# A transformer layer on one core: one pair of loads moved from the end of a stage to its eighth weight block, and the last two tiles of the program accumulated output tile by output tile

## What is computed

```python
h = _ln(x) * (1.0 + sc1) + sh1
x = x + g1 * _gqa_attn(h, wq, wk, wv, wo)     # 16 heads, 4 of keys and values
h = _ln(x) * (1.0 + sc2) + sh2
x = x + g2 * _mlp(h, w1, b1, w2, b2)          # gelu, 512 -> 2048 -> 512
```

## Time and profile before

| | |
|---|---|
| median of 3 runs | 1415.4 us (1413.36 to 1415.44) |
| the profiled execution, its own time | 1418.17 us |
| its span, first to last instruction | 1416.2 us |
| PE busy | 1381.6 us, 98% of the span |
| DVE, ACT, POOL busy | 881.1, 763.5, 641.7 us |

### The profile page before, as it was taken

The page is one execution under the profiler, slowest core; times in us unless marked ns, Lnnn a source line. Parts: engine busy times, 40 slices in busy tenths (PEclk is TensorE's granted clock), DMA queues, the critical chain, the costliest instruction groups (busy, mean ns, idle before and its releaser), DMA issues.

```text
span 1416.2 us, 19196 instructions
## 1 busy us (share of the span) xinstructions
PE 1381.6 (98%) x6681; PEld 991.2 (70%) x6681; DVE 881.1 (62%) x1481; ACT 763.5 (54%) x1375; POOL 641.7 (45%) x279
## 2 busy tenths in 40 slices
PE   6999999999999999999999999899999999999998
PEld 4655565665656566565567878788888888888886
DVE  3687787686777768677665565755475355733243
ACT  6377758576675856667756556534443344422221
POOL 3067687685867768587810085412032010311012
PEclk9999999999999999999999999999999999999999
DMA  8332222423233242323259685476662865546523
GB/s 285 88 90 59 67 92 82 123 78 106 57 91 96 83 117 80 110 57 87 78 165 266 137 277 152 156 253 193 179 193 66 303 189 164 155 156 195 149 82 119
DMA packets 163438, 193.85 MB, mean 137 GB/s; under 512 B 59960, under 2 KB 84552, under 8 KB 163344
## 3 DMA queue, kind: packets, MB, share of 16 engines
q1 hardware_dynamic: 163344, 192.64, 45.3%
HBM read 108.91 MB, written 40.93 MB: 106 GB/s over the span
## 4 chain that ended last, share of the span: by engine, by line
PE 82%; DVE 6%; SPq 3%; DMA 3%; ACT 2%; POOL 2%; issue 1%; DVEq 0%; ACTq 0%; POOLq 0%
PE acc L2388 18%; PE proj_bank L1183 13%; PE turn L2375 9%; PE key_bank L1267 8%; PE pv_bank L1276 7%; PE row_bank L1254 7%; PE up L2375 7%; PE up L1645 4%; PE acc L2339 3%; DVE neg_max L994 2%; PE sum_bank L1286 2%; SPq L559 2%; DMA gate_now<-gate_scratch 1%; POOL probs_sum L689 1%; PE proj_bank L1193 1%
## 5 line engine op out<-in xcount | busy, mean ns | idle before, releaser
L994 DVE TENSOR_REDUCE neg_max<-row_bank 128x1 f32<-128x512 f32 x512 | 337.7, 684 | 139.1 <-PE row_bank L1254 135.2
L818 ACT ACTIVATE probs<-key_bank 128x512 f32<-128x512 f32 x512 | 299.7, 598 | 159.4 <-PE key_bank L1267 149.0
L689 POOL TENSOR_TENSOR probs_sum<-probs_sum,probs 128x2048 f32<-128x2048 f32 x62 | 285.6, 4607 | 14.1 <-ACT probs L818 7.3
L2388 PE MATMUL acc<-w_t,hidden 128*128 128x512 f32 x1152 | 269.4, 390 | 0.3 <-DVE hidden L2231 0.3
L2388 PEld LDWEIGHTS acc<-w_t,hidden 128*128 128x128 f32 x1152 | 215.8, 188 | 46.7 <-DVE hidden L2231 1.7
L1267 PE MATMUL key_bank<-q_stack,k_stack 128*128 128x512 f32 x512 | 217.4, 428 | 3.3 <-ACT probs L818 2.8
L1254 PE MATMUL row_bank<-k_stack,q_stack 96*128 96x512 f32 x512 | 203.3, 408 | 4.4 <-DVE neg_max L994 2.9
L689 POOL TENSOR_TENSOR probs_sum<-probs 128x2048 f32<-128x2048 f32 x31 | 142.6, 4600 | 81.7 <-ACT probs L818 81.7
L1839 POOL TENSOR_TENSOR y<-y,resid 128x512 f32<-128x512 f32 x30 | 41.4, 1416 | 264.9 <-DVE y L2152 264.9
L1267 PEld LDWEIGHTS key_bank<-q_stack,k_stack 128*128 128x128 f32 x512 | 96.1, 188 | 83.3 <-issue 46.9
L1254 PEld LDWEIGHTS row_bank<-k_stack,q_stack 96*128 96x128 f32 x512 | 96.3, 188 | 38.9 <-DVE neg_max L994 17.1
(11 more groups left out here) (219 smaller groups left out, 1890.1 us busy)
## 6 DMA issues: line engine op xcount, KB each, us to landing
ring<-w1s_scratch SPq DMA_DIRECT2D x168, 256.0 KB, 3.7
q_stack<-spare SPq DMA_DIRECT2D x384, 64.0 KB, 2.0
hid_scratch<-spare SPq DMA_DIRECT2D x36, 256.0 KB, 4.9
spare<-hid_scratch SPq DMA_DIRECT2D x36, 256.0 KB, 2.7
xa<-in_x_dram SPq DMA_DIRECT2D x8, 1024.0 KB, 10.0
resid<-in_x_dram SPq DMA_DIRECT2D x8, 1024.0 KB, 7.2
x_scratch<-resid SPq DMA_DIRECT2D x8, 1024.0 KB, 4.5
spare<-in_L_cond_w_dram SPq DMA_DIRECT2D x32, 256.0 KB, 3.3
```

What stands on the lines that cost most here:

```text
L689: nc.gpsimd.tensor_tensor(probs_sum[:, :, :], first_in[:, :, :], probs[kt][:, :, :], ALU.add).then_inc(added, 1)
L818: nc.scalar.activation(probs[kt][:, r, :], key_bank[r % 2][:, :], ACT.Exp).then_inc(exp_done, 1)
L994: nc.vector.tensor_reduce(out=neg_max[:, g % 2, i:i + 1], in_=row_bank[(g + i) % 2][:, :], op=ALU.max, axis=AX.X, negate=True).then_inc(ro ...
L2388: last = nc.tensor.matmul(acc[tt][:, :], hidden[n % 2][i][:, tt * P:tt * P + P], w_t[:, j, 2 + k, :], start=(own == 0 and m == 0), stop=(o ...
```

## The change

There are two edits. First, `load_out_parts(0)` is issued by SP in the iteration j = 8 of `plain`, behind `store_block(4)` and ahead of the load of block 9; before, it was issued when all blocks had been turned. Second, the last two hidden tiles of the program (m = 14 and 15) are no longer added one after the other to all four output tiles: for each output tile the three passes of m = 14 and then of m = 15 are issued. For this, tile 15 gets a buffer of its own (`mixed[0]`, which holds no live data by then), and DVE takes tiles 0 and 1, and then takes and finishes tile 2, and takes and finishes tile 3.

```diff
@@ on_sync, plain
                     if j < STORES_REST:
                         store_block(j - 4)
-                    elif j >= TURN_FROM:
+                    if j == 8:
+                        sp.wait_ge(x1_stored, B * 16)
+                        load_out_parts(0)
+                    if j >= TURN_FROM:
                         turn_halves(1, (j - TURN_FROM,))
                 cross_weights(sp, NJ - 1)
                 turn_halves(1, range(NJ - TURN_FROM, TT))
-                sp.wait_ge(x1_stored, B * 16)
-                load_out_parts(0)
@@ on_scalar, b_high
-                hidden_free(c, NJ + m)
-                nc.scalar.activation(hidden[m % 2][0][:, :], b_tile[n % 4], ACT.Copy).then_inc(pair_hi, 1)
+                if c == B // 2 - 1 and m == NJ - 1:
+                    act.wait_ge(product_done, product_no(c, JP - 1, NQ - 1) + 1)
+                else:
+                    hidden_free(c, NJ + m)
+                nc.scalar.activation(b_hidden(c, m)[0], b_tile[n % 4], ACT.Copy).then_inc(pair_hi, 1)
@@ on_vector, pair
                 if not has_next:
-                    take_acc(2 * c + 1)
+                    take_acc(2 * c + 1, range(POOL_TILES))
                     for tt in range(POOL_TILES, TT):
+                        take_acc(2 * c + 1, (tt,))
                         add_last(2 * c + 1, tt)
@@ on_tensor
+            def last_products(c):
+                for tt in range(TT):
+                    for m in (NJ - 2, NJ - 1):
+                        tile = b_hidden(c, m)
+                        if tt == 0:
+                            pe.wait_ge(pair_split, pair_no(c, NJ + m))
+                        for n, (i, k) in enumerate(PASSES):
+                            last = nc.tensor.matmul(acc[tt][:, :], tile[i][:, tt * P:tt * P + P], w_t[:, w_slot(m), 2 + k, :],
+                                                    start=False, stop=(m == NJ - 1 and n == 2))
+                    last.then_inc(acc_ready, 1)
```

More of the change, by code:

```diff
@@ L134 @@
 COMBINED = ("U2", "U3", "C22", "C21", "C12")
[L135 removed]
+SECOND_SP = "S0 O0 S1 X3 S2 T20 T21 T22 T23 S3 T30 T31 T32 T33 S4 S5 S6 S7 R0 R1 R2 R3 R4 R5 R6 R7"
 SECOND_POOL = "S1 P2 S2 S3 S4 P3 S5 S6 S7 B1"
@@ L1518, in x_words, with b_hidden @@
             return xb_words[:, tt, :, :] if s % 2 == 0 or s == 1 else xs_words[tt // 2][:, tt % 2, :, :]
+        def b_hidden(c, m):
+            is_last = c == B // 2 - 1 and m == NJ - 1
+            return [mixed[0][:, i, :] if is_last else hidden[m % 2][i][:, :] for i in range(2)]
         def product_no(c, jp, q):
@@ L1687, in turn_halves @@
             def turn_halves(s, tiles=range(TT)):
-                if s > 1:
+                if s > 1 and tiles[0] == 0:
                     sp.wait_ge(joined, (s - 1) * 8)
@@ L1771, in second @@
                     elif step[0] == "T":
-                        turn_halves(int(step[1]))
+                        turn_halves(int(step[1]), (int(step[2]),))
                     elif step[0] == "R":
@@ L2144, in hidden_low, with take_acc @@
                                         ALU.subtract).then_inc(hid_split, 1)
-            def take_acc(b):
-                if b > 0:
+            def take_acc(b, tiles=range(TT)):
+                if b > 0 and tiles[0] == 0:
                     dve.wait_ge(out_stored, b * 16)
-                dve.wait_ge(gate_loaded, b * 16 + 16)
-                for tt in range(TT):
+                if tiles[0] == 0:
+                    dve.wait_ge(gate_loaded, b * 16 + 16)
+                for tt in tiles:
                     dve.wait_ge(acc_ready, b * TT + (tt + 1))
@@ L2230, in b_low @@
                 dve.wait_ge(pair_hi, pair_no(c, NJ + m))
-                nc.vector.tensor_tensor(hidden[m % 2][1][:, :], b_tile[tile_of(m) % 4], as_f32(hidden[m % 2][0][:, :]),
-                                        ALU.subtract).then_inc(pair_split, 1)
+                high, low = b_hidden(c, m)
+                nc.vector.tensor_tensor(low, b_tile[tile_of(m) % 4], as_f32(high), ALU.subtract).then_inc(pair_split, 1)
             def plain():
@@ L2393, in pair_product, with w_slot @@
                     last.then_inc(pair_down, 1)
+            def w_slot(m):
+                n = tile_of(m)
+                return n // 2 + (0 if n % 2 else JP)
+            def last_products(c):
[8 more added lines that the diff above has]
+                    last.then_inc(acc_ready, 1)
             def plain():
@@ L2425, in pair @@
                 pair_product(c, NJ - 1, NJ - 1)
-                for m in range(NJ):
-                    n = tile_of(m)
-                    pair_product(c, NJ + m, n // 2 + (0 if n % 2 else JP))
+                for m in range(NJ if has_next else NJ - 2):
+                    pair_product(c, NJ + m, w_slot(m))
+                if not has_next:
+                    last_products(c)
             sequences(pe, plain, second, pair)
```

## The result

The changed kernel takes 1420.99 us (median of 6 runs, 1419.14 to 1422.13). The kernel before, run beside it, takes 1415.42 us (6 runs, 1413.36 to 1416.23). The ratio is 1.0039, with a 95% interval from 1.0027 to 1.0052: slower, by about 5.6 us. The forecast was 1417.0, with a range that ended at 1419.6. The profiled execution took 1422.02 us, with a span of 1420.0.

A forecast was written before the change was run, and what follows sets the result against it. PE, at work for 98% of the span, was taken to bound the kernel. Wait +4.0, clock +1.9, boundary -1.75, second stage -1.5, tail -1.05 make +1.6 us; on the median 1415.4 this gives 1417.0, range 1412.4 to 1419.6.

The forecast's parts named there:

- PE waits 4.0 us: At block 8: gate and residual ahead of weights and transposes make PE wait 4.0 us; bounds 1.8 and 4.9.
- POOL's contention: At block 8's join and shift: POOL's residual additions delay DVE, up to 2.2 us more, 1.3 taken within PE's wait.
- The clock: Behind PE's wait at block 8: a lower granted clock costs 1.9 us; bounds 0 and 1.9.
- The boundary: Between first and second stage: DVE's hidden low parts no longer run beside POOL's additions, gain 1.75 us; lower bound 1.0.
- The second stage: Second MLP stage: POOL is ahead and its sums no longer hold ACT's gelu, 1.5 us more gain; bounds 0 and 1.6.
- The tail: Behind PE's last product: only one taking and one addition are left, gain 1.05 us; bounds 0.5 and 1.1.
- The cheap early load: Rival at block 8: join by 771.5, wait only 1.8 us, clock holds, 2.5 us faster at 1412.9; chance 0.17.
- The slower rival: Second stage keeps its end and block 8's wait is 4.9 us: +4.0 us, 1419.4; chance 0.22.
- the wait above 5.2 us: At block 8: PE's wait exceeds 5.2 us, another way to a slower kernel; chance 0.05.

The follow-up runs named there:

- Experiment 7: Changed kernel with only the gate loaded early and the residual at its old place: 1416.09 us against 1416.22 for the kernel before, ratio 0.9996.
- experiment 5: Changed kernel with POOL's four residual additions held back until block 8's low parts are made: 1419.52 us, ratio 1.0021 to the kernel before.
- experiment 3: Changed kernel with PE's four transposes of block 9 issued 13 times, giving PE work during the wait: 1418.96 us, ratio 1.0016 to the kernel before.
- experiment 1: The two edits apart, ratios to the kernel before: the end alone (second edit, loads at their old place) 1.0000; early loads alone with the old end 1.0036.
- experiments 1 and 8: Beside experiment 1, the eighth: changed kernel with loads in the iteration of block 11, old end 0.9985, new end again 0.9978, to the kernel before.
- the repeat: The changed kernel once more, beside the kernel before on another chip: 1419.99 us, ratio 1.0034.
- experiment 2: Changed kernel with gate and residual loaded in the iteration of block 11, not 8: 1413.67 us against 1416.25 for the kernel before, ratio 0.9978.

## Why the prediction was wrong

**The step that failed** is "PE waits 4.0 us", above all the landing in it. I had the mechanism right: these two loads, this join, this shift, this product. But the wait was 5.68 us, above the upper bound of 4.9 that I gave it. I put 10.0 us between the gate's issue (762.36) and the last transpose's landing (772.4). It took 11.9: 761.91 to 773.83, in parts

- the residual landed 8.37 us after the gate's issue, where I had 7.6;
- block 9's two pieces landed 2.5 us behind it, where I had 1.4 (0.7 each);
- the transposes landed 1.1 us behind those, where I had 1.0.

The join, which the earlier execution would have started at 767.98, started at 773.92. It was 5.94 us late and not 3.96. The upper bound was too narrow for a simple reason: only POOL's contention moved it, and the landing stood in it at the value taken. I worked that out from one row of each kind and 0.7 us for each piece of 0.25 MB. The load's own row of 8.2 us, which I put aside, was the nearer one: block 9's first piece took 8.9 us. Experiment 7 shows that this piece price is too low as a price of delay: a gate of 0.25 MB ahead made the load behind it 2.4 us slower. Why (the gate is read from its scratch in another form than a weight, and a stored block goes ahead) was not taken apart.

**POOL's contention** was right: 1.3 us taken, 1.2 us in the join (2.00 against 0.79), and 1.14 less wait in experiment 5. The shift itself was not held (0.14 us). The late join, less the slack of 1.28 us, plus these 1.2 us, is 5.9 us, near the 5.68 measured.

**The clock** was wrong in size: +1.9 taken, which was also my upper bound, 3.1 measured, of which experiment 3 shows 2.85 to be the clock's. Behind the longer wait the lower level held for 6.8 us, through all of one product and part of the next. I had carried over, as the upper bound too, the cost of the fall behind a wait of 1.8 us. That cost itself is nearer 1.6: the same two products take 7.2 us from start to start in the kernel before (906.76 to 913.98) and 5.6 in the kernel with the end alone (906.12 to 911.73).

**The boundary** had the right mechanism, with `h` at 0.64 us, near the 0.7 I said: 1.75 taken, 1.55 measured. But the profile of before is a poor base for it. In experiment 1's kernel with the end alone the loads are at their old place too, and the same stretch, from the gelu of block 15 to the first of sequence 1, is 9.06 us there, not 9.70:

```profile
819.46 0.66 ACT L1932 ACTIVATE up<-up,bias_cols 128x512 f32<-128x512 f32 x1 [2.74 <-PE up L1650]
828.52 0.66 ACT L1932 ACTIVATE up<-up,bias_cols 128x512 f32<-128x512 f32 x1 [3.99 <-PE up L1650]
```

Against the changed kernel's 8.15 that is a gain of 0.9 us.

**The second stage** was right: 1.5 taken, 1.45 measured. The eight transposes start 23.31 us after the stage's first gelu, where it was 24.82 (24.83 with the end alone). The gain appears at the earlier of the stage's two waits for `hidden`, before and after:

```profile
887.99 3.01 PE L2339 MATMUL acc<-w_t,hidden 128*128 128x512 f32 x12 [1.76 <-DVE hidden L2143]
```

```profile
893.30 3.02 PE L2350 MATMUL acc<-w_t,hidden 128*128 128x512 f32 x12 [0.33 <-DVE hidden L2152]
```

**The tail** was right in the profile, 1.05 taken and 1.08 measured, but its share of the time is not resolved (experiments 1 and 8).

So the sum with measured terms is 5.7 + 3.1 - 1.55 - 1.45 - 1.1 = +4.7 in place of +1.6. Of the 3.1 us between them 1.7 are the wait, 1.2 the clock and 0.2 the boundary. With the boundary counted from the kernel with the end alone, 0.9 us, the sum is +5.3.

**The rivals.** The cheap early load fell by its own condition: the join came at 773.9 and not by 771.5. The Trainium skill's sentence in "DMA: Bandwidth & Descriptors", section "Queues, rings and completion order", that completion is not first in, first out, was behind it. In this case the residual (770.28), block 9's pieces (772.04, 772.76) and the transposes (773.40, 773.83) landed in the order of issue, so the trace shows no overtaking. The slower rival gave the right side, for the smaller part of its cause: the second stage did not keep its end, the wait above 5.2 us did it, to which I gave 0.05.

**Open.** The sum of the steps is 4.7 us, the medians say 5.6 and, in the repeat, 5.0. Part of this lies in the profile of before, which at 1418.17 is 2.8 us above the median of 1415.4. At the boundary it is 0.64 us longer than the profile with the end alone. And two products behind its wait at 905 lost 1.6 us to the clock, which in eleven of the twelve profiles of the experiments, with the same wait of about 1.75 us, are not lost. The changed kernel's profile has this loss too, so it cancels between the two profiles, but it would not between medians if it came more often in one kernel; how often it comes was not measured. Counted from the profile with the end alone, and with the tail's 1.1 us, the steps are 8.8 - 0.9 - 1.4 - 1.1 = +5.4 us. The 1.4 is the fall of the wait for `hidden` at 888, from 1.71 us there to 0.33. The same count for experiment 2 gives 0.9 - 0.8 - 1.3 - 1.1 = -2.3 us, where the medians have -2.6. So the steps account for the times to a few tenths, by one profile of each kernel. Why the clock costs 2.1 us in one profile and 2.85 in another, behind waits of the same length, stays open.

## What to carry to other kernels

A load that is moved forward is paid for by what stands behind it in its DMA queue. Add to the landing of those DMAs every instruction that stands behind their first user in the lists of its engine, up to the bound engine; the same 1.25 MB cost 5.7 us of wait in iteration 8, and none right behind them in iteration 11 or 12, where no normalisation is queued behind the join. Check the profile that a forecast starts from against a second one of the same kernel or of a near one: at one boundary two such profiles differed by 0.64 us. Bound a landing by more than one row, and price a wait of the matmul engine with its clock behind it: here 5.7 us of wait became 8.8. A version with the loads at block 11 or 12 is 0.22% faster than the kernel before, where the one at block 8 is 0.39% slower.

## What the runs showed that I had not expected

- A 0.25 MB gate in front of a 256 KB load raised its landing from 3.0 to 5.4 us; gate and residual together raised it to 9.1.
- Behind the wait of about 1.76 us at 901 to 913 the clock fell in the profiles of before, of the changed kernel (not in its repeat) and of block 12, and not in the eleven other profiles, whose wait is as long.
- Fifty-two small transposes, 5.84 us of PE work, were enough in experiment 3 to keep the granted clock at its higher level through the wait.
- The same two 16-bit copies of DVE take 0.8 us alone, and 1.9 to 2.9 beside POOL's additions.
